# The gap of an eigenvalue turn: from two matmuls to a matmul and a subtraction, and its product with A from VectorE to GpSimd

## The reference

```
w, V = eigh(X);  L = V diag(log clip(w)) V^T        # per 32x32 matrix
L = gamma * (L - mean over the batch of L) + beta
Y = V' diag(exp w') V'^T                            # of L, again per matrix
x = x + Y
```

## Time and profile before

| | |
|---|---|
| runs | 9319.95, 9320.89, 9331.5 us (median 9320.89) |
| profiled execution | 9336.33 us, span 9334.6 us |
| PE busy / DVE / ACT / POOL, share of the span | 88% / 59% / 42% / 21% |
| `eigen` | about 247 us to 3780 us of the span, 384 slots |

### The profile page before, as it was taken

One profiled execution on the slowest core, in us unless ns is written; L12 is line 12 of the kernel. 1 busy time (PEld: TensorE's weight loads), 2 busy tenths in 40 slices (PEclk: granted clock), 3 DMA queues, 4 the chain that ended last, 5 costly groups with the idle time before them and its releaser, 6 DMA issues. The chain is left out here.

```text
span 9334.6 us, 604193 instructions
## 1 busy us (share of the span) xinstructions
PE 8227.5 (88%) x266349; PEld 4441.4 (48%) x266732; DVE 5465.7 (59%) x15245; ACT 3963.6 (42%) x7646; POOL 1955.6 (21%) x2042
## 2 busy tenths in 40 slices
PE   3899999999998779478759999999999999999998
PEld 2677777777776667367632222222222222222222
DVE  4677777777776447533245555555555555555554
ACT  3455555555554335144424343444343444343443
POOL 0555555555555235100000000000000000000000
PEclk9999999999999889689869999999999999999999
DMA  0000000000000000000000000000000000000000
GB/s 36 1 0 0 0 0 0 0 0 0 0 0 0 0 0 0 2 1 0 30 11 1 3 3 3 1 3 3 3 3 3 1 3 3 3 3 3 1 3 5
DMA packets 9761, 32.01 MB, mean 3 GB/s; under 512 B 1525, under 2 KB 3130, under 8 KB 9274
## 3 DMA queue, kind: packets, MB, share of 16 engines
q1 hardware_dynamic: 9274, 26.02, 0.7%
HBM read 17.63 MB, written 8.39 MB: 3 GB/s over the span
## 5 line engine op out<-in xcount | busy, mean ns | idle before, releaser
L1932 DVE MAX8 w_best<-psum 128x8 f32<-128x128 f32 x8192 | 1724.4, 283 | 1289.5 <-PE psum L1465 1244.0
L1915 ACT ACTIVATE w_exp<-psum 128x512 f32<-128x512 f32 x2048 | 1221.0, 596 | 2387.0 <-PE psum L1474 2384.7
L1484 PE MATMUL psum<-w_exp,w_v 128*32 128x512 f32 x4096 | 2096.1, 610 | 1.0 <-ACT w_inverse L1517 1.0
L499 PE MATMUL psum<-e_prod_u,e_j 32*32 32x64 f32 x49152 | 769.4, 216 | 30.3 <-ACT e_prod_u L579 25.1
L499 PEld LDWEIGHTS psum<-e_prod_u,e_j 32*32 32x32 f32 x49152 | 707.6, 106 | 182.5 <-issue 182.5
L1474 PE MATMUL psum<-w_q,w_k 99*128 99x512 bf16 x2048 | 789.8, 386 | 1.4 <-ACT w_q L1499 1.4
L1465 PE MATMUL psum<-w_k,w_q 96*128 96x512 bf16 x2048 | 628.0, 389 | 156.2 <-DVE w_best L1932 114.0
L1484 PEld LDWEIGHTS psum<-w_exp,w_v 128*32 128x32 f32 x4096 | 277.0, 108 | 757.2 <-issue 757.2
L653 POOL TENSOR_TENSOR e_diag<-odd,e_eye 128x512 f32<-128x512 f32 x384 | 488.2, 1271 | 561.7 <-PE psum L473 523.6
L547 ACT ACTIVATE e_square<-e_off 128x512 bf16<-128x512 f32 x384 | 242.0, 630 | 844.2 <-POOL e_off L657 844.2
L1465 PEld LDWEIGHTS psum<-w_k,w_q 96*128 96x128 bf16 x2048 | 121.5, 97 | 993.4 <-issue 990.0
(11 more groups left out here) (282 smaller groups left out, 11628.4 us busy)
## 6 DMA issues: line engine op xcount, KB each, us to landing
odd<-in_x SPq DMA_DIRECT2D x1, 8192.0 KB, 23.3
even<-in_x SPq DMA_DIRECT2D x1, 8192.0 KB, 23.6
out<-w_t SPq DMA_DIRECT2D x16, 512.0 KB, 2.6
w_hid<-in_fc SPq DMA_DIRECT2D x2, 256.0 KB
w_wo<-in_wo SPq DMA_DIRECT2D x8, 8.0 KB
w_wq<-in_wq SPq DMA_DIRECT2D x1, 64.0 KB
w_wk<-in_wk SPq DMA_DIRECT2D x1, 64.0 KB
w_wv<-in_wv SPq DMA_DIRECT2D x1, 64.0 KB
```

Source lines behind the costliest of these rows:

```text
L499: last = nc.tensor.matmul(halves(e.pair[:, k // HALF, :])[rows, :, to], e.j[rows, cols], e.prod_u[rows, :, cols], start=True, stop=True)
L1484: nc.tensor.matmul(banks[7][slot(j), :], w.v[:, kt, 4 * g + j, :], w.exp[x % 4][:], start=(kt == 0), stop=(kt == KT - 1)).then_inc(s.weigh ...
L1915: nc.scalar.activation(w.exp[x % 4][:], banks[4 + x % 2], ACT.Exp).then_inc(s.exp_done, 1)
L1932: last = nc.vector.max(w.best[:, i, o, :], banks[o // 4][:, P * (o % 4):P * (o % 4) + P])
```

## The change

The second gap matmul (L473) and its constant go. The matmul L472 alone fills the gap bank with the column sums. VectorE subtracts the row sums into a new SBUF tile `e_gap`, ScalarE squares that tile, and GpSimd multiplies it with A. VectorE's row sums of the next tile stand ahead of the damping sum. In `load_weights` two semaphores become one with the same order of work.

```diff
 PE   def gaps(m, which, first=False):
-                hold(pe, rows_ready, diag_rows_at(m))
-                if not first:
-                    hold(pe, damped, m)
-                nc.tensor.matmul(banks[GAP], e.block_ones[:], e.diag[:], start=True, stop=False)
-                nc.tensor.matmul(banks[GAP], e.minus_ident[:], over_columns(e.diag_rows[:]), start=False, stop=True)\
-                    .then_inc(gap_done, 1)
-                hold(pe, square_ready, m + 1)
+                hold(pe, diag_ready, m + 1)
+                if not first:
+                    hold(pe, gap_ready, m)
+                nc.tensor.matmul(banks[GAP], e.block_ones[:], e.diag[:], start=True, stop=True).then_inc(gap_done, 1)
+                hold(pe, square_ready, m + 1)
+                if not first:
+                    hold(pe, damped, m)
 ACT  if has(0):
-                    act.wait_ge(gap_done, tau + 1)
-                    nc.scalar.activation(e.gap_sq[:], banks[GAP], ACT.Square).then_inc(gap_squared, 1)
+                    act.wait_ge(gap_ready, tau + 1)
+                    if has(AT_ANGLE):
+                        act.wait_ge(damped, tau - AT_ANGLE + 1)
+                    nc.scalar.activation(e.gap_sq[:], e.gap[:], ACT.Square).then_inc(gap_squared, 1)
 DVE  def rows(m, first=False):
-                    dve.wait_ge(gap_done, m)
+                    dve.wait_ge(gap_ready, m)
 DVE  if has(0):      (behind e_x)
+                    dve.wait_ge(gap_done, tau + 1)
+                    dve.wait_ge(rows_ready, diag_rows_at(tau))
+                    if has(AT_ANGLE):
+                        dve.wait_ge(gap_squared, tau - AT_ANGLE + 1)
+                        dve.wait_ge(weighed, tau - AT_ANGLE + 1)
+                    nc.vector.tensor_tensor(as_matrices(e.gap[:]), as_matrices(banks[GAP]), over_columns(e.diag_rows[:]),
+                                            ALU.subtract).then_inc(gap_ready, 1)
+                if has(AHEAD):
+                    rows(tau + 1)
+                if has(0):
                     dve.wait_ge(gap_squared, tau + 1)
-                    if has(AT_ANGLE):
-                        dve.wait_ge(angle, tau - AT_ANGLE + 1)
-                    nc.vector.tensor_tensor(e.weighed[:], e.a_at(tile_of(j, 0)), banks[GAP], ALU.mult).then_inc(weighed, 1)
                     dve.wait_ge(damp_done, tau + 1)
                     nc.vector.tensor_tensor(e.damped[:], e.gap_sq[:], banks[DAMP], ALU.add).then_inc(damped, 1)
-                if has(AHEAD):
-                    rows(tau + 1)
 POOL def masks(m, t, first=False):
                     hold(pool, gap_done, m)
+                    hold(pool, rows_ready, diag_rows_at(m - 1))
 POOL (at the end of the body)
+                if has(0):
+                    hold(pool, gap_ready, tau + 1)
+                    if has(AT_ANGLE):
+                        hold(pool, angle, tau - AT_ANGLE + 1)
+                    nc.gpsimd.tensor_tensor(e.weighed[:], e.a_at(tile_of(j, 0)), e.gap[:], ALU.mult).then_inc(weighed, 1)
```

More of the change, by code:

```diff
@@ L186, in __init__ @@
         self.block_ones = sb("e_block_ones", [P, P])
-        self.minus_ident = sb("e_minus_ident", [P, P])
         self.damp = [sb(f"e_damp{n}", [P, P], BF16) for n in range(2)]
@@ L208, in open_tiles @@
         self.prod_u = sb("e_prod_u", [P, 2, W])
+        self.gap = sb("e_gap", [P, W])
         self.square = sb("e_square", [P, W], BF16)
@@ L267, in _ @@
             nc.vector.tensor_reduce(e.eye[:], mem.ident[:].rearrange(folded, j=S), AX.X, ALU.add).then_inc(copied, 1)
-            nc.vector.tensor_scalar(e.minus_ident[:], mem.ident[:], -1.0, None, ALU.mult).then_inc(copied, 1)
             nc.vector.tensor_reduce(e.ramp[:, 0:1], triangle[:], AX.X, ALU.add).then_inc(copied, 1)
-            dve.wait_ge(copied, 3)
+            dve.wait_ge(copied, 2)
             nc.vector.tensor_scalar(e.not_eye[:], e.eye[:], -1.0, 1.0, ALU.mult, ALU.add).then_inc(copied, 1)
@@ L276, in _ @@
             for n, value in enumerate((FIRST_DAMP, LATER_DAMP)):
+                dve.wait_ge(copied, 5 + 3 * n)
+                nc.vector.tensor_scalar(spare[:], mem.ident[:], KAPPA / value, None, ALU.mult).then_inc(copied, 1)
                 dve.wait_ge(copied, 6 + 3 * n)
-                nc.vector.tensor_scalar(spare[:], mem.ident[:], KAPPA / value, None, ALU.mult).then_inc(copied, 1)
+                nc.vector.tensor_tensor(spare[:], spare[:], e.block_ones[:], ALU.add).then_inc(copied, 1)
                 dve.wait_ge(copied, 7 + 3 * n)
-                nc.vector.tensor_tensor(spare[:], spare[:], e.block_ones[:], ALU.add).then_inc(copied, 1)
-                dve.wait_ge(copied, 8 + 3 * n)
                 nc.vector.tensor_scalar(e.damp[n][:], spare[:], value, None, ALU.mult).then_inc(copied, 1)
@@ L284, in _ @@
                 nc.vector.tensor_scalar(e.damp_ident[n][:], mem.ident[:], value, None, ALU.mult).then_inc(copied, 1)
-            dve.wait_ge(copied, 14)
+            dve.wait_ge(copied, 13)
             dve.wait_ge(summed, 1)
@@ L289, in _ @@
                 .then_inc(copied, 1)
-            dve.wait_ge(copied, 15)
+            dve.wait_ge(copied, 14)
             nc.vector.tensor_reduce(e.mirror_rows[:], e.mirror[:].rearrange(folded, j=S), AX.X, ALU.add).then_inc(copied, 1)
@@ L418, in eigen @@
                                                                             "e_rows_ready"))
-        gap_done, damp_done, gap_squared, damped = (sem(n) for n in ("e_gap_done", "e_damp_done", "e_gap_squared",
-                                                                     "e_damped"))
+        gap_done, damp_done, gap_ready, gap_squared, damped = (sem(n) for n in ("e_gap_done", "e_damp_done", "e_gap_ready",
+                                                                                "e_gap_squared", "e_damped"))
         weighed, log_taken, inverse, angle, eye_added = (sem(n) for n in ("e_weighed", "e_log_taken", "e_inverse", "e_angle",
@@ L1093, in sem @@
             return ctx.enter_context(nc.semaphore(name))
-        cleared, loaded, turned, copied, selected = (sem(n) for n in ("w_cleared", "w_loaded", "w_turned", "w_copied",
-                                                                      "w_selected"))
+        cleared, loaded, turned, copied = (sem(n) for n in ("w_cleared", "w_loaded", "w_turned", "w_copied"))
         gates = ctx.enter_context(nc.sbuf_tensor("gates", [EXPERTS + 1, P], F32))
@@ L1122, in _ @@
                                     compare_op=ALU.not_equal, fill=1.0, base=-DH, pattern=[[-SLOT, 4], [0, SLOT]],
-                                    channel_multiplier=1).then_inc(selected, 1)
-            n = 1
+                                    channel_multiplier=1).then_inc(cleared, 1)
+            n = len(pads) + 3
             for stack, parts in ((w.stack_q, PARTS_Q), (w.stack_k, PARTS_K)):
@@ L1128, in _ @@
                     nc.gpsimd.affine_select(out=to, in_=to, compare_op=ALU.not_equal, fill=1.0, base=0,
-                                            pattern=[[-DH, HEADS], [-1, DH]], channel_multiplier=1).then_inc(selected, 1)
+                                            pattern=[[-DH, HEADS], [-1, DH]], channel_multiplier=1).then_inc(cleared, 1)
                     n += 1
-            pool.wait_ge(selected, n)
-            nc.gpsimd.tensor_copy(w.ident[:], mem.ident[:]).then_inc(selected, 1)
-            pool.wait_ge(selected, n + 1)
+            pool.wait_ge(cleared, n)
+            nc.gpsimd.tensor_copy(w.ident[:], mem.ident[:]).then_inc(cleared, 1)
+            pool.wait_ge(cleared, n + 1)
         @block.sync
```

## The result

The changed kernel takes 9195.02 us (median of 4 runs, 9192.57 to 9202.49), the kernel before 9326.15 (4 runs); the ratio is 0.9861, 95% interval 0.9844 to 0.9878: 131 us less. The profiled execution took 9202.49 us, 133.8 less than that of before.

The account below looks back on a forecast made before the run. TensorE's instruction stream was taken to bound steady slots at 8.40 us. Steady slots -111 and mended slots +12 took the profiled 9336.33 to 9237 us; for the median, 9320.9 - 102 = 9219 us, range 9100 to 9590.

Parts of the forecast that it names:

- What goes from TensorE: Steady slots: L473's two passes go, 0.86 us a slot, so TensorE alone would need 7.54 us for 8.40.
- What is late next: Steady slots: the earlier mask on GpSimd meets VectorE's sum and `e_x`; by the shared port `e_x` is held 1.12 us.
- rival 3: No shared port, the holds seen before have another cause: 287 us less, 9034 us; chance 0.07.
- The mask's request: GpSimd's mask asks for the port 5.78 to 5.94 us after the subtraction, 0 to 0.14 behind the sum.
- Sum of the cycle: Steady slot from one subtraction to the next: 5.80 + 0.56 + 1.12 + 0.60 = 8.08 us, 0.32 saved.
- the 0.08 for ScalarE's second wait: Between subtraction and square: 0.72 us, and 0.08 more for the square's second wait, 0.80 in all.
- The mended slots: 32 slots with GpSimd on the path: +1.22 for the product, -0.86 on TensorE, +12 us in all (-8 to +30).
- Rival 1: The mask asks before the sum, so sum and `e_x` are both held: slots 9.0 to 9.2 us, 9577 us; chance 0.23.
- Rival 2: VectorE keeps the port from the sum to `e_x`: slots between 7.54 and 8.0 us, 9142 us; chance 0.20.
- Rival 4: The holds and one more wait (late ScalarE, falling clock) eat the rest of the gain: 9310 to 9330 us; chance 0.05.

Follow-up runs that it names:

- e1: Changed kernel, but Exp writes into the idle mending bank of PSUM in slots not mended, so `e_x` has one SBUF input: 9053.2 us, ratio 0.9697.
- e3: Changed kernel with GpSimd's `e_off` of the next tile moved ahead of the A copy: 9006.2 us, ratio 0.9644.
- e4: Changed kernel with GpSimd's `e_off` ahead of `e_diag` and the A copy last, behind the product: 8966.6 us, ratio 0.9604.
- e7: Changed kernel with the first damping matmul issued three times instead of once: 9224.2 us, ratio 0.9880.
- e9: Changed kernel with one tiny VectorE instruction more, ahead of the sum into A: 9228.5 us, ratio 0.9882.
- e10: e9 with GpSimd's two waits ahead of the mask exchanged, the gap matmul's last: 9453.8 us, ratio 1.0123.
- e2: Changed kernel, but GpSimd's masks of the next tile also wait for `e_x` of this slot: 9495.4 us, ratio 1.0172.
- e6: Changed kernel with VectorE's row sums of the next tile put back behind the damping sum: 9223.4 us, ratio 0.9877.
- e8: The kernel before, not the changed one, with GpSimd's order of e4: 9273.7 us, ratio 0.9934.

## Why the prediction was right

- What goes from TensorE: two passes, 0.86 us a slot. e1, e3 and e4 show the 7.54 forecast for TensorE alone, as 7.55; e7 shows that it isn't what sets 7.98.
- What is late next: the step that decided. Without rows 5 the sum ends at 287 us less (rival 3), and 131 were measured. The order sum, mask, `e_x`, `e_off` is the forecast one, and the holds of 0.55 and 1.12 are those read from before. The mask's request was put at 5.78 to 5.94 behind the subtraction and came at 5.89, but partly by luck, as two errors offset each other: the square came 0.08 sooner than the working has it, and the product started 0.99 behind `e_j` (1509.16 to 1510.15), not 0.86. Without these 0.13 it would have asked at 5.76, 0.06 behind the sum.
- Sum of the cycle: 8.08 forecast, 7.98 measured. The term mis-sized is the 0.08 for ScalarE's second wait; the square starts 0.72 behind the subtraction, so that wait, already met, cost nothing here. The other 0.02 are rounding in the chain (5.70 to the sum L628, for 5.80 with the 0.08); the hold and what follows it fit (0.56 + 1.12 + 0.60 = 2.28 forecast, 2.29 measured). A steady slot saves 0.41 and not 0.32, 348 x 0.09 = 31 us more; less the 7 by which the mended slots cost more, this is most of the step from 102 to 131.
- The mended slots: +12 forecast, +19 measured, in the range given. GpSimd's path grew by 1.25 us as forecast (1.22), and the granted clock fell from 0.86 to 0.83; that the clock makes up the other 7 us is not shown.
- Rival 1 was real, but 0.18 us away in most slots and 0.09 in a sixth of them, for 0 to 0.14 forecast; e9 and e10 together took more than that and tipped it. The rows could order the two requests only because GpSimd's second wait lay on the mask's side: it cost 0.17 us (0.44 behind the bank's end for 0.27), all of the margin but 0.01. Rival 2 asked whether VectorE keeps the port for `e_x`, due 0.05 us after the sum lets go; it doesn't, the waiting mask gets in (`e_x` held in 279 of 281 slots). Rival 3 is refuted by e1. Rival 4 did not come: `e_off` of the slot before ends at 1508.40 (1506.68 + 1.72) and `e_square` starts at 1508.43, right behind the square, and the clock is 1.00 from 1500 to 1668 us.
- The rule on the shared read port that the prediction cites (the Trainium skill, SBUF — State Buffer, Who interferes with whom) agrees with every timeline shown here; e1 shows its condition, two SBUF inputs, by moving one input only. By the recorded durations the port is free a little before the end of the instruction that has it: 0.55 us into the 0.68 of the sum, 1.12 into the 1.27 of a mask.

## What to carry to other kernels

When a matmul that paced a loop goes, ask which instruction starts by its semaphore, and what then runs beside it: list VectorE's instructions with two SBUF inputs against GpSimd's that read SBUF, and look for durations above the shortest of the same instruction, which busy shares hide. Move one of the two to a gap of its engine (e4), or an operand to PSUM (e1); a wait that keeps them apart can cost more than the hold (e2). A pipeline that depends on such a race can lose a microsecond a slot when one of the two comes 0.17 us sooner (e10), so read the margin of the race as well as the mean.

## What was not expected of the hardware

One race for the port can give one loop two steady patterns: slots of 6.90 and 9.20 us in turn in e6, and in e7 slots of 7.98 for most of the run and of 9.2 and 6.9 at its end.

How soon GpSimd starts behind the semaphore that it waits for last differs with what stands between: in most slots 0.27 us with nothing behind that wait (rows 4, e10), 0.44 with a second wait behind it (1512.63, the bank's end, to 1513.07), 0.59 with two (e2). The number of waits is not all of it: with the same two waits the mask starts after 0.35 in e3 and e4, and in a sixth of the changed kernel's slots, and with the one wait after 0.18 in e8. What makes this difference was not tested.
